# A fused cross-attention and feed-forward kernel: other first maxima for batch 0, and another order in the last step

## The reference

```python
Q = heads(layernorm(x) @ w_q.T)            # 16 heads of width 8
K, V = heads(ctx @ w_k.T), heads(ctx @ w_v.T)
scores = Q K^T / sqrt(8);  scores = where(mask, scores, -inf)
x = x + softmax(scores) V @ w_o.T
h = silu(layernorm(x) @ wg.T) * (layernorm(x) @ wu.T)   # hidden width 384, weights int32 / 127
x = x + h @ wd.T
```

## Time and profile before

| | |
|---|---|
| median of 3 runs | 191.45 us (189.88 to 256.48) |
| profiled execution | 189.59 us, span 187.80 us |
| mean granted TensorE clock over the span | 0.964 of full speed |
| busy: PE, DVE, ACT, POOL | 168.6, 133.3, 107.2, 67.0 us |
| first head of batch 0's maxima starts on PE | 19.28 us |
| step 0 starts (first `scores` of batch 0) | 31.67 us |
| step 1 starts | 48.17 us |
| last step starts | 149.99 us |
| the turn of batch 7's normalised x | 178.14 us |

### The profile page before, as it was taken

How to read it: one execution, slowest core, us unless ns; L and a number is a source line. 1 busy time by engine, 2 the same in 40 slices (tenths; PEclk the granted TensorE clock), 3 DMA queues, 4 the chain that set the end, 5 groups by cost and what they waited for, 6 DMA issues and landing times.

```text
span 187.8 us, 4293 instructions
## 1 busy us (share of the span) xinstructions
PE 168.6 (90%) x1636; PEld 105.9 (56%) x1636; DVE 133.3 (71%) x308; ACT 107.2 (57%) x226; POOL 67.0 (36%) x114
## 2 busy tenths in 40 slices
PE   5858998599996999999999999998999999997883
PEld 4648554254452556557656655754565466655863
DVE  6853897676799578968896886899689815425441
ACT  5432014657794488577867785777577577533030
POOL 6233605918427533950674085004100500310100
PEclk9996999659999699999999999999999999999999
DMA  4739797491096029405930870394000000000100
GB/s 147 261 97 183 210 179 231 134 185 24 8 245 94 3 63 213 68 0 155 173 47 12 232 133 0 93 212 67 3 30 2 3 2 28 5 28 0 31 2 28
DMA packets 17381, 17.06 MB, mean 91 GB/s; under 512 B 1520, under 2 KB 15984, under 8 KB 16688
## 3 DMA queue, kind: packets, MB, share of 16 engines
q1 hardware_dynamic: 16896, 16.12, 37.4%
q10 hardware_dynamic: 464, 0.67, 1.3%
HBM read 9.24 MB, written 7.34 MB: 88 GB/s over the span
## 4 chain that ended last, share of the span: by engine, by line
PE 54%; DVE 17%; issue 15%; POOL 6%; ACT 3%; DMA 2%; ACTq 1%; SPq 1%; POOLq 0%
PE pv_bank L336 12%; PE score_bank L276 9%; DVE neg_max L742 9%; PE pv_bank L403 5%; PE max_bank L293 4%; PE ffn_bank L389 4%; PE ffn_bank L377 3%; DMA ctx_all<-ctxT 2%; PE ffn_bank L380 2%; PE prep_bank L315 2%; PE prep_bank L307 2%; PE post_bank L365 2%; PE post_bank L352 2%; DVE stats L811 1%; PE prep_bank L311 1%
## 5 line engine op out<-in xcount | busy, mean ns | idle before, releaser
L742 DVE TENSOR_REDUCE neg_max<-max_bank 128x2 f32<-128x512 f32 x128 | 82.0, 685 | 17.9 <-PE max_bank L293 17.3
L566 ACT ACTIVATE probs<-score_bank 128x512 f32<-128x512 f32 x128 | 70.0, 597 | 20.7 <-PE score_bank L276 20.7
L293 PE MATMUL max_bank<-k_ops,q_ops 49*128 49x256 bf16 x256 | 44.0, 280 | 2.8 <-DVE neg_max L742 2.8
L276 PE MATMUL score_bank<-q_ops,k_ops 51*128 51x256 bf16 x256 | 43.7, 280 | 1.9 <-ACT probs L566 1.1
L336 PE MATMUL pv_bank<-probs,v_ops 128*32 128x256 f32 x512 | 35.2, 390 | 0.0
L276 PEld LDWEIGHTS score_bank<-q_ops,k_ops 51*128 51x128 bf16 x256 | 19.8, 95 | 22.1 <-ACT probs L566 9.9
L293 PEld LDWEIGHTS max_bank<-k_ops,q_ops 49*128 49x128 bf16 x256 | 17.4, 95 | 8.3 <-DVE neg_max L742 5.6
L990 POOL CAST max_parts<-neg_max 128x16 bf16<-128x16 f32 x14 | 2.8, 198 | 51.7 <-DVE neg_max L742 51.7
L336 PEld LDWEIGHTS pv_bank<-probs,v_ops 128*32 128x32 f32 x512 | 14.7, 110 | 11.2 <-issue 5.4
L403 PE MATMUL pv_bank<-ident_bf 128*128 128x128 bf16 x212 | 18.5, 242 | 1.9 <-POOL ident_bf L1020 1.9
L403 PEld LDWEIGHTS pv_bank<-ident_bf 128*128 128x128 bf16 x212 | 15.0, 110 | 5.9 <-issue 3.6
(11 more groups left out here) (117 smaller groups left out, 221.0 us busy)
## 6 DMA issues: line engine op xcount, KB each, us to landing
k_ops<-k_rows SPq DMA_DIRECT2D x7, 384.0 KB, 4.8
q_ops<-q_rows SPq DMA_DIRECT2D x7, 384.0 KB, 6.1
k_rows<-kq_parts SPq DMA_DIRECT2D x8, 192.0 KB, 2.1
q_rows<-kq_parts SPq DMA_DIRECT2D x8, 192.0 KB, 2.2
k_rows<-kq_parts SPq DMA_DIRECT2D x8, 128.0 KB, 2.1
q_rows<-kq_parts SPq DMA_DIRECT2D x8, 128.0 KB, 2.1
out<-y SPq DMA_DIRECT2D x8, 128.0 KB, 2.1
x_all<-x SPq DMA_DIRECT2D x1, 768.0 KB, 6.6
```

Source lines behind the costliest of these rows:

```text
L276: mm = pe.matmul(score_bank[k % 2][:, t * S:(t + 1) * S], rows(k_ops, b, ROWS)[:, k, t * P:(t + 1) * P], rows(q_ops, b, ROWS)[:, k, :], st ...
L293: mm = pe.matmul(max_bank[k % 2][:, t * S:(t + 1) * S], rows(q_ops, b, MAX_ROWS)[:, k, t * P:(t + 1) * P], rows(k_ops, b, MAX_ROWS)[:, k, ...
L566: act.activation(probs[:, k % RING].rearrange("p t s -> p (t s)"), score_bank[k % 2][:, :], ACT.Exp, scale=SCALE).then_inc(probs_ready, 1)
L742: dve.tensor_reduce(neg_max[:, b % 2, :, k], max_bank[k % 2][:, :].rearrange("p (t s) -> p t s", t=TT), AX.X, ALU.max, negate=True).then_i ...
```

## The change

It has two halves.

*Batch 0's maxima.* They no longer wait for the DRAM round trip. The weights are regrouped (`w_heads`) so that a projection puts each head into one of four groups of 32 rows, head k in group k % 4. DVE builds `head_rows`, four columns of zeros and ones that select the 8 rows of one head in a group, ACT copies the projected k four times with one of these columns as scale (`k_of_heads`), and q once. `first_max_scores` then multiplies 32 rows of q by 32 rows of k in float32 for each half of the tokens, and adds the mask by a matmul one row deep. It uses four banks in turn, the two of the maxima and the two of the scores. The 49-row matmuls of batch 0 and the `keep_warm` between them are gone. The loads of `ctx` change place: batch 0's goes out on ACT's queue as the second, and that of batches 2 and 3 goes out on SP after `spread_shift(0, 0)`. DVE's `memset` of the second q buffer moves to POOL, ACT's fill of the second k buffer moves behind `copy_kq(2)`, and the first scores wait for all 16 maxima.

*Last step and epilogue.* `hidden` is double-buffered, batch 7's chain goes ahead of the down projections of batches 5 and 6, the blocks of `keep_warm` are gone, `normalise_x1(6)` is on DVE in place of POOL, the last down projection takes the chunks as they come, and y of batch 7 is stored in two halves.

SP's queue, the first scores and the end of the stores:

```diff
-            sp.dma_start(ctx_all[:, 0], ctxT[:, 0]).then_inc(ctx_in[0], 16)
             sp.dma_start(x_all[:, 0], x[:, 0]).then_inc(x_in[0], 16)
...
-            sp.wait_ge(q_filled[0], 1)
-            sp.wait_ge(q_bounced[0], 16 * PARTS)
-            for g in range(2):
-                half_from_dram(sp, 0, g)
-            sp.dma_start(ctx_all[:, 2:4], ctxT[:, 2:4]).then_inc(ctx_in[2], 16)
...
+            sp.wait_ge(q_filled[0], 1)
+            from_dram(sp, 0, 0)
...
             from_dram(sp, 1, 0)
+            spread_shift(0, 0)
+            sp.dma_start(ctx_all[:, 2:4], ctxT[:, 2:4]).then_inc(ctx_in[2], 16)
             sp.dma_start(wff_int[:, :, :], wff_in).then_inc(wff_loaded, 16)
-            spread_shift(0, 0)
             sp.dma_start(ctx_all[:, 4:B], ctxT[:, 4:B]).then_inc(ctx_in[3], 16)
...
-            for b in range(B - 3, B):
+            for b in range(B - 3, LAST):
                 store(b)
-            sp.wait_ge(stored, 16 * B)
+            for t in range(TT):
+                sp.wait_ge(y_done, B + t)
+                sp.dma_start(out[:, LAST, t], y[:, LAST, t]).then_inc(stored, 16)
+            sp.wait_ge(stored, 16 * (B + 1))
...
                 if t == 0:
+                    if n == 0:
+                        pe.wait_ge(k_spread[0], 32)
+                        pe.wait_ge(q_spread[0], 16)
+                        pe.wait_ge(max_done, HEADS)
                     if k % HALF == 0:
                         pe.wait_ge(shift_spread[b][k // HALF], 16)
```

PE in the prologue:

```diff
+            def first_max_scores(k):
+
+                if k == 0:
+                    pe.wait_ge(q_heads_ready, 1)
+                    pe.wait_ge(ones_ready, 1)
+                    pe.wait_ge(mask0_ready, 1)
+                    pe.wait_ge(k_heads_ready, 1)
+                if k == 3:
+                    pe.wait_ge(k_heads_ready, OF_GROUP)
+                if k >= 4:
+                    pe.wait_ge(max_done, k - 3)
+                r = GROUP * (k % 4)
+                to = first_max_bank[k % 4]
+                for t in range(TT):
+                    pe.matmul(to[:, t * S:(t + 1) * S], q_heads[r:r + GROUP, t * P:(t + 1) * P],
+                              k_heads[r:r + GROUP, k // 4], start=True, stop=False)
+                    mm = pe.matmul(to[:, t * S:(t + 1) * S], ones_row[r:r + 1, :], mask0[r:r + 1, :],
+                                   start=False, stop=True)
+                mm.then_inc(max_scores_ready, 1)
+
+            def project_for_heads(side, to, of):
+                pe.wait_ge(w_heads_ready, side + 1)
+                return pe.matmul(to, w_heads[:, side], of, start=True, stop=True)
...
-            project_k(0, score_bank[0][:, 0:S]).then_inc(k_proj, 1)
-            project_k(1, max_bank[0][:, 0:S]).then_inc(k_proj, 1)
-            keep_warm(16, pv_bank)
-            turn_xn1(0, score_bank[1])
-            keep_warm(6, pv_bank)
+            ctx_wait(pe, 0)
+            project_for_heads(0, score_bank[1][:, 0:S], ctx_all[:, 0]).then_inc(k_heads_proj, 1)
+            project_k(0, pv_bank[:, 0:S]).then_inc(k_proj, 1)
+            project_k(1, prep_bank[:, 0:S]).then_inc(k_proj, 1)
+            keep_warm(8, max_bank[0])
+            turn_xn1(0, score_bank[0])
+            keep_warm(6, max_bank[0])
+            pe.wait_ge(xn1_t_ready, 1)
+            project_for_heads(1, post_bank[:, 0:S], xn1_t[:, :]).then_inc(q_heads_proj, 1)
             project_q(0, ffn_bank[:, 0:S]).then_inc(q_proj, 1)
+            keep_warm(4, max_bank[0])
+            first_max_scores(0)
+            turn_xn1(1, post_bank)
+            first_max_scores(1)
+            first_max_scores(2)
+            project_q(1, post_bank[:, 0:S]).then_inc(q_proj, 1)
+            first_max_scores(3)
+            first_max_scores(4)
+            first_max_scores(5)
             pe.wait_ge(wvo_loaded, 16)
-            project_v(0, post_bank)
-            turn_xn1(1, prep_bank)
-            keep_warm(6, pv_bank)
-            project_q(1, score_bank[1][:, 0:S]).then_inc(q_proj, 1)
-            pe.wait_ge(v_ready, 1)
-            project_v(1, post_bank)
-            keep_warm(40, pv_bank)
+            pe.wait_ge(q_rest, 1)
+            project_v(0, ffn_bank)
+            first_max_scores(6)
+            first_max_scores(7)
             pe.wait_ge(k_rest, 2)
-            for k in range(HEADS):
-                max_head(0, k)
-                keep_warm(4, pv_bank)
-                if k == 8:
-                    turn_xn1(2, prep_bank)
-                if k == 10:
-                    pe.wait_ge(v_ready, 2)
-                    turn_max(0, 0, post_bank)
-                if k == 12:
-                    pe.wait_ge(xn1_t_ready, 3)
-                    project_k(2, prep_bank[:, 0:S])
-                    project_q(2, prep_bank[:, S:2 * S]).then_inc(kq_proj, 1)
+            project_v(1, prep_bank)
+            first_max_scores(8)
+            turn_xn1(2, pv_bank)
+            first_max_scores(9)
+            first_max_scores(10)
             pe.wait_ge(q_rest, 2)
+            turn_max(0, 0, post_bank)
+            first_max_scores(11)
+            first_max_scores(12)
+            pe.wait_ge(xn1_t_ready, 3)
+            project_k(2, pv_bank[:, 0:S])
+            project_q(2, pv_bank[:, S:2 * S]).then_inc(kq_proj, 1)
+            first_max_scores(13)
+            first_max_scores(14)
+            first_max_scores(15)
```

PE in the last step:

```diff
+            def project_down_by_chunk(b, to):
+                for c in range(CH):
+                    pe.wait_ge(hidden_done, CH * b + c + 1)
+                    for t in range(TT):
+                        mm = pe.matmul(to[t][:, 0:P], hidden[:, b % 2, c, t * P:(t + 1) * P], wff[:, 2 * CH + c],
+                                       start=c == 0, stop=c == CH - 1)
+                        if c == CH - 1:
+                            mm.then_inc(down_done, 1)
...
+            times_v(b, 2)
             both(b, 14)
-            times_v(b, 2)
-            project_gate_up(b - 1, 0, max_bank[1])
+            pe.wait_ge(hidden_done, CH * (b - 2) + 1)
+            project_gate_up(b - 1, 0, max_bank[0])
             times_v(b, 3)
-            project_gate_up(b - 1, 1, ffn_bank)
+            pe.wait_ge(hidden_done, CH * (b - 2) + 2)
+            project_gate_up(b - 1, 1, max_bank[1])
+            turn_pv(b)
+            pe.wait_ge(hidden_done, CH * (b - 2) + 3)
+            project_gate_up(b - 1, 2, ffn_bank)
+            turn_attn(b)
             pe.wait_ge(max_t_ready, 2 * B)
-            project_gate_up(b - 1, 2, prep_bank)
-            turn_pv(b)
-            turn_attn(b)
-            pe.wait_ge(y_done, b - 1)
-            project_down(b - 1, 0, max_bank[0])
-            project_down(b - 1, 1, max_bank[0])
+            project_down(b - 2, 0, prep_bank)
             project_attn(b)
-            keep_warm(44, pv_bank)
+            project_down(b - 2, 1, prep_bank)
+            pe.wait_ge(probs_ready, HEADS * B)
             turn_xn2(b)
-            keep_warm(6, pv_bank)
-            pe.wait_ge(probs_ready, HEADS * B)
             project_gate_up(b, 0, score_bank[0])
             project_gate_up(b, 1, score_bank[1])
-            project_gate_up(b, 2, max_bank[1])
-            keep_warm(12, pv_bank)
-            project_down(b, 0, ffn_bank)
-            project_down(b, 1, ffn_bank)
+            pe.wait_ge(hidden_done, CH * (b - 1) + 1)
+            project_gate_up(b, 2, max_bank[0])
+            pe.wait_ge(pv_copied, B)
+            project_down(b - 1, 0, pv_bank)
+            project_down(b - 1, 1, pv_bank)
+            project_down_by_chunk(b, (ffn_bank, max_bank[1]))
```

ACT and DVE in the prologue:

```diff
+            def k_of_heads(j):
+                if j == 0:
+                    act.wait_ge(head_rows_ready, 1)
+                    act.wait_ge(k_heads_proj, 1)
+                act.activation(k_heads[:, j], score_bank[1][:, 0:S], ACT.Copy, scale=head_rows[:, j:j + 1])\
+                    .then_inc(k_heads_ready, 1)
+
             act.dma_start(wkq[:, :, :], wkq_in).then_inc(wkq_loaded, 16)
+            act.dma_start(ctx_all[:, 0], ctxT[:, 0]).then_inc(ctx_in[0], 16)
+            act.dma_start(mask0_u8[:, :], mask[0:1, :].broadcast_to([P, S])).then_inc(mask0_loaded, 16)
...
+            part1(0, 0, k_proj, pv_bank[:, 0:S], 0, k_part1)
+            k_of_heads(0)
+            part1(0, 1, k_rest, kq_rest[:, 0:S], 0, k_part2)
+            for j in range(1, OF_GROUP):
+                k_of_heads(j)
+            part1(1, 0, k_proj, prep_bank[:, 0:S], 0, k_part1)
+            copy_xn1_t(0, score_bank[0])
+            act.wait_ge(q_heads_proj, 1)
+            act.activation(q_heads[:, :], post_bank[:, 0:S], ACT.Copy).then_inc(q_heads_ready, 1)
+            part1(0, 0, q_proj, ffn_bank[:, 0:S], S, q_part1)
+            part1(1, 1, k_rest, kq_f[:, 0:S], 0, k_part2)
+            copy_xn1_t(1, post_bank)
+            part1(0, 1, q_rest, kq_rest[:, S:2 * S], S, q_part2)
+            part1(1, 0, q_proj, post_bank[:, 0:S], S, q_part1)
...
+            dve.wait_ge(ident_ready, 1)
```

(29 more changed lines are left out.)

168 lines of the change are left out of this document (85 added, 83 removed).

## The result

| | before | after |
|---|---|---|
| median, us | 191.38 (4 runs, 189.88 to 256.48) | 200.22 (4 runs, 199.53 to 201.27) |
| profiled execution, us | 189.59 | 199.63 |
| its span, us | 187.8 | 197.8 |
| mean granted clock | 0.964 | 0.896 |

The change makes the kernel slower: the ratio of after to before is 1.049, with an interval of 1.040 to 1.059. (Ratios here leave out executions that were disturbed, which medians do not, so the two can differ by a per cent or so.) I had forecast 191.6 in a range of 186.5 to 196.0. In the profiled executions, step 0 starts at 48.05 in place of 31.67 (+16.4) and the last step at 164.38 in place of 149.99 (+14.4). From there to the end it takes 33.4 us in place of 37.8 (-4.4). So 189.6 + 14.4 - 4.4 = 199.6. The prologue cost 9.4 more than the 5.0 I had costed.

What follows compares the result with a forecast made beforehand. PE was taken as busy nine tenths or more in most of the run, with gaps in the first third and at the end. 189.6 + 5.0 (prologue) - 3.0 (end) = 191.6 us, range 186.5 to 196.0.

Steps and rivals of the forecast that it cites:

- the 5.0 I had costed: Prologue, up to the start of step 0: net loss of 5.0 us, from 1.8 to 6.5 at the extremes.
- the price of the heads: Prologue, batch 0's maxima on PE: 1.07 us a head instead of 0.65, 17.1 us for 16.
- rival 3: Prologue: heads run at half clock, their 19.8 us taking 39.6, for 207.9 us in all; chance 0.12.
- rival 1: Prologue: heads in different groups of 32 rows overlap and DVE sets the pace, 186.3 us in all; chance 0.08.
- First head: Prologue: batch 0's first head starts at 12.3 instead of 19.28, about 7 us earlier.
- The `ctx` load: Prologue: PE waits 3.8 us (2.7 at least) for batches 2 and 3's context, ahead of `project_k(2)`.
- The clock behind that wait: Prologue, after PE's wait for the context: half clock costs 1.3 us, with 0 and 1.7 as ends.
- What the steps give back: Step 0: batch 3's x turns 5.5 us later, not 6.2, and a missing half-clock stretch gives back 0.5.
- The end: Last step and epilogue: three savings of 2.1, 1.8 and 0.6, together 4.5 us.
- The clock behind it: End, after PE's idle wait before batch 7's x turns: half clock costs 1.5 us, expected three times in four.
- net 3.0: Last step and epilogue: 4.5 us saved less 1.5 given to the clock, 3.0 saved.

Runs made afterwards that it cites:

- the experiment: The changed kernel with the context load of batches 2 and 3 issued on SyncE's queue before batch 1's stores to the scratch: 197.73 us.

## Why the prediction was wrong

**The step that failed is the price of the heads.** I took full clock for them, 1.07 us each and 17.1 for 16, and gave half clock (rival 3) a chance of 0.12 because PE would stream without a gap. It streamed without a gap, and the clock fell 3.6 us into the heads. Rival 3 named the lack of depth, and I let the busy time outweigh it. The experiments decide it: the same program with 128 rows kept 1.00 until a wait at 38.4. Whether the clock counts rows or the use of row groups as such, no run separates. The work from the first head to the last was 19.8 in the forecast. It took 31.6 (13.19 to 46.9 less the wait of 2.1), of which 28.0 at half clock. The Trainium skill, "TensorE: Matmul & The Clock Gate", section "Why this matters for your kernels", puts the loss of the clock down to stretches in which PE is idle. No row of these stretches shows such a one (2.00 of 2.00), so here the measurement decides against that as the only cause.

**Rival 3's own price, 207.9, was too high** by 8. The first 3.6 us of heads ran at full clock, and at my rates what was left when the clock fell would have taken 32.4 and took 28.0, with the overlap at the borders.

**The overlap (rival 1)** was right as a mechanism and wrong as a bound. It did not make DVE the pace, since most heads stood alone, or issued all four of their matmuls before the next. In pairs, at full clock, a head took 0.65, below DVE's 0.69 of the earlier trace rows, and there PE did wait for DVE, 0.71 at 16.6.

**First head:** 12.3 forecast, 13.19 measured. The projection of q ahead of it took 0.86 (11.77 to 12.63) where 0.44 is full clock. In two runs where it took 0.43 the first head came at 11.95 and 12.13.

**The `ctx` load:** 3.8 forecast, 2.1 measured, and the experiment gives 2.1 back. The load landed 6.0 after the turn, as costed (6.1); PE reached the wait 3.8 after the turn and not 2.3, because its two heads ran at half clock. **The clock behind that wait** (1.3) had nothing left to lose. Over 128 rows it did fall behind the same wait, for 3.4 us, so this term was right in kind.

**What the steps give back:** I took 0.7 ahead of the turn of batch 3's x and 0.5 behind it. Ahead of it it was 1.0 (16.4 at step 0's start, 15.4 at the turn). Behind it, step 0 gave nothing back: step 1 starts 15.9 later (64.05 for 48.17). The other 1.5 down to 14.4 is no gain of the change. Step 1 took 17.54 in the kernel before and 16.02 in the changed one, and only the former was at half clock in it, from 61.8 to 65.2. The two traces of the end's half alone, with the same prologue as before, have no such fall, so it belongs to that execution. Its windows, kernel before:

```profile
60.00:64.00 4.00, 3.70 (x35) 2.01 (x35) 2.19 (x8) 1.60 (x4) 2.27 (x3) 0.73 0.01 4
64.00:66.00 2.00, 2.00 (x26) 0.86 (x24) 1.24 (x2) 1.00 (x2) 0.61 (x3) 0.69 0.00 0
```

**The end:** 4.5 saved, 4.4 measured, and the turn of batch 7's x at 24.3 after the step's start where I had 24. The clock behind it, 1.5 at three in four, was not lost in this execution. Where it fell in others, the end from that turn took 10.5 to 10.8 in place of 9.1. Of the eleven profiled executions with this end, seven had the fall, where I had said three in four. Over all executions, with the fall and without it, the end's half alone saved 2.8 and 3.2 (188.83 to 186.02, 189.03 to 185.82), near the net 3.0 of the forecast.

## What to carry to other kernels

In this kernel the depth of the matmuls was part of what TensorE's clock answered to. Before full-depth work is replaced by work in row groups, cost it at half clock as well as at full, however well it fills the engine, and read the clock's row before the busy share. If row groups are used, issue the matmuls of different groups in turn, and keep matmuls of another depth from between them. If the maxima need all rows, bring a one-row mask to the same depth. Measure the halves of a change apart: here one was worth 1.5 to 2.2% and hid behind the other's 8%.

## What was not expected of the hardware

- PE, busy 2.00 of every 2.00 us from 12 to 38 and mostly with float32 matmuls 32 rows deep, was granted 0.50 from 16.8 on, and until 57.8, in all 41 us. With two groups side by side it was 27 us, with four full-depth bf16 matmuls ahead of each head 58 us. Over 128 rows it was 1.00 throughout the heads, but for 3.4 us behind a wait of 2.37 in one run.
- A change from 128 rows to one and back cost 0.30 us at full clock, beside the matmuls' 0.54. The mask over 128 rows of 1/128 cost 0.11 (a half of 0.54 for 0.43 without it) where the one-row mask cost 0.41.
- A matmul of 256 float32 columns takes about as long over 32 rows as over 128 (0.70 for two in both), and two in different groups of rows take no longer than one.
- The same wait of 2.35 us ahead of the same matmul was followed by half clock in some executions and not in others. Why is open.
